# Layer 1's norm and the reading of the top-k maxima move from VectorE to GpSimd in a four-stage block on one core

## The reference

```
def _L1_xattn_ref(query, key, value, Wq, Wk):
    ...
    scores = jnp.einsum('bhqa,bhka->bhqk', q, k) * SCALE
    top_vals = jax.lax.top_k(scores, TOP_K)[0]
    cutoff = top_vals[..., -1:]
    masked = jnp.where(scores >= cutoff, scores, -jnp.inf)
    w = jax.nn.softmax(masked, axis=-1)
    e = jnp.einsum('bhqk,bhka->bhqa', w, v)
...
x = x + _L0_xattn_ref(_layernorm(x, axis=-1), ctx_1024, ctx_1024, mask_BxS2_bf1, ...)
x = x + _L0_ffn_ref(_layernorm(x, axis=-1), ...)
x = x + _L1_xattn_ref(_layernorm(x, axis=-1), ctx_1024, ctx_1024, L1_xattn_Wq, L1_xattn_Wk)
x = x + _L1_ffn_ref(_layernorm(x, axis=-1), ...)
```

## Time and profile before

| | us |
|---|---|
| median of three runs | 620.87 |
| the profiled execution | 620.93 |
| its span, first to last instruction | 618.9 |
| VectorE busy | 513.5 |
| TensorE busy | 443.1 |
| ScalarE busy | 280.4 |
| GpSimd busy | 255.2 |

### The profile page before, as it was taken

How to read it: one execution, slowest core, us unless ns; L and a number is a source line. 1 busy time by engine, 2 the same in 40 slices (tenths; PEclk the granted TensorE clock), 3 DMA queues, 4 the chain that set the end, 5 groups by cost and what they waited for, 6 DMA issues and landing times.

```text
span 618.9 us, 10023 instructions
## 1 busy us (share of the span) xinstructions
PE 443.1 (72%) x2321; PEld 334.7 (54%) x2321; DVE 513.5 (83%) x3073; ACT 280.4 (45%) x781; POOL 255.2 (41%) x388
## 2 busy tenths in 40 slices
PE   5879978687877877637777757765977876556355
PEld 4458755466664764524656535654755655445244
DVE  5845776947884998999875999999999999989971
ACT  2213431321232424522674758676567877443521
POOL 5400110500131255342672765675486776444611
PEclk9999995957677668755876779789568978566555
DMA  8500000000000000000000000000000000000000
GB/s 294 215 1 1 2 2 0 0 1 1 2 0 1 2 1 0 2 1 2 5 2 5 5 2 2 10 2 1 6 5 6 3 9 3 5 5 5 5 1 8
DMA packets 5929, 9.54 MB, mean 15 GB/s; under 512 B 744, under 2 KB 4976, under 8 KB 5616
## 3 DMA queue, kind: packets, MB, share of 16 engines
q1 hardware_dynamic: 5584, 8.35, 3.8%
q10 hardware_dynamic: 288, 0.56, 0.3%
HBM read 7.86 MB, written 1.05 MB: 14 GB/s over the span
## 4 chain that ended last, share of the span: by engine, by line
PE 38%; DVE 37%; ACT 11%; issue 9%; POOL 3%; DMA 1%; SPq 0%; ACTq 0%; DVEq 0%; POOLq 0%
DVE area_b L921 10%; DVE top L913 9%; PE psM L1261 5%; PE psM L1066 4%; PE psM L1211 3%; PE psM L1203 3%; ACT mparts L557 2%; DVE mxc L928 2%; PE psS L1034 2%; PE psM L1198 2%; PE psM L1139 2%; DVE d L691 2%; PE psT L1055 2%; PE psT L1247 2%; PE psS L1037 2%
## 5 line engine op out<-in xcount | busy, mean ns | idle before, releaser
L913 DVE MAX8 top<-area_b 128x8 f32<-128x77 f32 x768 | 112.4, 221 | 0.0
L921 DVE MATCH_REPLACE8 area_b<-top,area_b 128x77 f32<-128x77 f32 x512 | 106.9, 222 | 0.0
L307 POOL TENSOR_TENSOR rstd_m<-veps_m,expo 128x4 f32<-128x4 f32 x8 | 8.1, 1013 | 130.7 <-DVE veps_m L659 130.7
L1261 PEld LDWEIGHTS psM<-vblk,pT 128*128 128x128 f32 (+1 forms) x320 | 52.5, 256 | 11.6 <-issue 10.5
L1261 PE MATMUL psM<-vblk,pT 128*128 128x81 f32 (+1 forms) x320 | 53.9, 341 | 6.1 <-ACT pT L612 5.8
L1066 PE MATMUL psM<-vblk,pT 128*128 128x81 f32 (+1 forms) x320 | 49.1, 320 | 6.9 <-DVE x L712 3.4
L921 DVE MATCH_REPLACE8 area_b<-top,area_a 128x77 f32<-128x77 f32 x256 | 53.5, 224 | 0.0
L1066 PEld LDWEIGHTS psM<-vblk,pT 128*128 128x128 f32 (+1 forms) x320 | 47.5, 236 | 10.4 <-issue 10.1
L408 POOL TENSOR_TENSOR p<-area_b 128x1232 f32<-128x1232 f32 x15 | 41.9, 2793 | 21.8 <-issue 17.1
L1203 PE MATMUL psM<-w,y1T 128*128 128x512 f32 (+1 forms) x64 | 34.1, 624 | 20.0 <-ACT mparts L557 19.8
L1247 PE MATMUL psT<-consts,p 128*128 128x128 f32 (+1 forms) x160 | 34.3, 342 | 19.5 <-ACT pT L608 10.5
(11 more groups left out here) (220 smaller groups left out, 1074.9 us busy)
## 6 DMA issues: line engine op xcount, KB each, us to landing
area_a<-in_w1T SPq DMA_DIRECT2D x1, 2064.0 KB, 11.2
area_b<-in_w SPq DMA_DIRECT2D x1, 2048.0 KB, 15.7
x<-in_x SPq DMA_DIRECT2D x4, 256.0 KB, 6.8
out<-fin SPq DMA_DIRECT2D x16, 64.0 KB, 1.6
rows<-in_rows SPq DMA_DIRECT2D x1, 576.0 KB, 6.9
vblk<-in_vblk SPq DMA_DIRECT2D x1, 540.0 KB, 15.6
weights<-in_weights SPq DMA_DIRECT2D x1, 516.0 KB, 6.7
consts<-in_consts ACTq DMA_DIRECT2D x1, 392.5 KB, 4.0
```

The source lines that it names most:

```text
L913: ins = e.max(top[:, r, h], (left if r else scores_sb[t % RING])[:, h])
L921: ins = e.match_replace(left[:, h], top[:, r, h], (left if r else scores_sb[t % RING])[:, h], GONE)
L1261: ins = mm(pvs1[:, :, FIRST[c] * VE:FIRST[c] * VE + VB], pT1[0:w, c], vblk1[0:w, t // NJ, c, None, :].broadcast_to([w, COPIES, VB]), start ...
```

## The change

Four edits:

1. `top` has two buffers, by the tile's parity. `mxc` and the copies `free` and `ends` are gone. GpSimd's `dif` and `cut` read the maxima in `top` itself, and wait for the steps of the top-k. The first MAX8 of tile t waits for the cut subtraction of tile t-2 (`cut_set` at t-1), where it waited for the previous tile's copy.
2. The step `norm` of tiles 0 to 14 is GpSimd's. A new ScalarE step, `ncopy`, copies the product, 128 x 144, to `avs` in SBUF, and GpSimd raises the 16 sums to the power -1 (`inverse` holds -1) and multiplies. Tile 15 keeps VectorE's norm.
3. In ORDER, `ncopy@t` stands right before `norm@t`, and `free` and `ends` are taken out. All other steps stand as they stood.
4. GpSimd sets the constant `inverse` at the start.

```diff
-        top = sb("top", [P, TOPK // 8, H, 8])
-        mxc = sb("mxc", [P, RING, 2, H])
+        top = sb("top", [P, 2, TOPK // 8, H, 8])
...
+        avs = sb("avs", [P, H, VE])
+        inverse = sb("inverse", [P, H])
...
+            e.memset(inverse[:], -1.0).then_inc(s["constants_set"], 1)
...
                 def a():
-                    hold(e, s["S_read"], t + 1)
+                    hold(e, s["topk_step"], TOPK_STEPS * t + G)
                     hold(e, s["exp_set"], t)
-                    e.tensor_tensor(dif[:], scores_sb[t % RING][:], mxc[:, t % RING, 0, :, None].broadcast_to([P, H, KEYS]), ALU.subtract)\
+                    e.tensor_tensor(dif[:], scores_sb[t % RING][:], top[:, t % 2, 0, :, 0, None].broadcast_to([P, H, KEYS]), ALU.subtract)\
...
-                    hold(e, s["mx_copied"], t + 1)
-                    e.tensor_tensor(cut, scores_sb[t % RING][:], mxc[:, t % RING, 1, :, None].broadcast_to([P, H, KEYS]), ALU.subtract)\
+                    hold(e, s["topk_step"], TOPK_STEPS * t + TOPK_STEPS)
+                    e.tensor_tensor(cut, scores_sb[t % RING][:], top[:, t % 2, TOPK // 8 - 1, :, 7, None].broadcast_to([P, H, KEYS]), ALU.subtract)\
...
             def value(t):
+                def norm():
+                    hold(e, s["constants_set"], 7)
+                    hold(e, s["a_copied"], t + 1)
+                    e.tensor_tensor(rden1[:], avs[:, :, HD], inverse[:], ALU.pow).then_inc(s["a_den"], 1)
+                    hold(e, s["a_den"], t + 1)
+                    hold(e, s["x3_set"], t)
+                    e.tensor_tensor(att1.rearrange("p (h d) -> p h d", h=H), avs[:, :, 0:HD],
+                                    rden1[:, :, None].broadcast_to([P, H, HD]), ALU.mult).then_inc(s["a_norm"], 1)
...
                 def keep():
                     hold(e, s["S_ready"], t + 1)
-                    hold(e, s["S_read"], t + 1 - RING)
...
+            def value(t):
+                def aside():
+                    hold(e, s["a_made"], t + 1)
+                    hold(e, s["a_norm"], t)
+                    e.activation(avs[:], pv1, ACT.Copy).then_inc(s["a_copied"], 1)
+                return dict(ncopy=aside) if t < LASTT else {}
...
                         if r == 0:
-                            hold(e, s["mx_copied"], t)
+                            hold(e, s["cut_set"], t - 1)
                             hold(e, s["S_kept"], t + 1)
...
-                def free():
-                    hold(e, s["cut_set"], t + 1 - RING)
-                    hold(e, s["topk_step"], last(2))
-                    e.tensor_copy(mxc[:, t % RING, 0], top[:, 0, :, 0]).then_inc(s["S_read"], 1)
-
-                def ends():
-                    hold(e, s["topk_step"], last(2 * rounds - 1))
-                    e.tensor_copy(mxc[:, t % RING, 1], top[:, rounds - 1, :, 7]).then_inc(s["mx_copied"], 1)
```

## The result

| kernel | median us (range, runs) | ratio to before, 95% interval | profiled execution, its span |
|---|---|---|---|
| before | 620.44 (618.68 to 620.9, 4) | | 620.93, 618.9 |
| changed | 651.90 (650.41 to 656.38, 4) | 1.0525, [1.0469, 1.058] | 650.41, 648.6 |

The change costs 31.5 us by the medians and 29.7 us by the spans. 648 us was forecast, and 617 to 662 as the range. (One line of the change isn't in the diff ahead: TensorE's next product with the values waits for ScalarE's copy and no longer for the norm.)

A forecast was written before the change was run, and what follows sets the result against it. VectorE was taken to set the pace only in part, with GpSimd, ScalarE and TensorE nearly as late in fixed order. Terms 7.6 + 6.5 + 14.0 + 2.4 = 30.5 us, less an eighth, +27: 648 us, range 617 to 662.

The forecast's parts named there:

- The power: GpSimd's power of 128x16 in each norm of tiles 0 to 14: 2.87 us by the line through one and four columns.
- (b): Rival: the power costs about 1.0 us at 16 columns, as at four, giving 624 us; chance 0.12.
- What VectorE loses: Both small copies of the maxima and the norm of 15 tiles leave VectorE: 27.6 us of its time.
- The multiply and the copy: In each moved norm, GpSimd's multiply of 128x128 takes 0.45 us and ScalarE's copy of the product 0.30 us.
- Tiles 0 and 1: +7.6: Start of tile 4's top-k comes 7.6 us later: tile 1 +3.8, tile 0 +3.5, tile 2's new copy +0.3.
- Tiles 2 to 6: +6.5: Up to tile 7's cut: five norms add 17.0 us, less 10.5 of vanishing waits for VectorE.
- Tiles 7 to 11: +14.0: Each norm costs its 3.3 us less the slack between x3's add and ScalarE's sum; together 14.0 us.
- Tiles 12 to 14: +2.4: Loop from cut to cut becomes 21.5 us: +3.1 from tile 12 to 13, -0.7 from 13 to 14.
- The eighth: Estimated deduction from the 30.5 us sum, for idle time of ScalarE and GpSimd from 450 to 500 us; leaves +27.
- (a): Rival: VectorE sets the end and the queues absorb the norms; 604 us, or 596 if early norms hide too; chance 0.17.
- (c): Rival: only the loop from cut to cut counts, the queues have room for the rest; 619 us; chance 0.09.
- (d): Rival: TensorE, waiting more, keeps its lower clock from tile 7 on, adding some 10 us; 658 us; chance 0.08.

The follow-up runs named there:

- three lengths of it: Changed kernel with GpSimd's power over 4 of 16 columns, over all 16, or done twice: 623.52, 651.90 and 700.19 us.
- the one with tiles 0 to 6: Maxima read in place in all tiles, norm on GpSimd only in tiles 0 to 6 and on VectorE in 7 to 14: 629.46 us, ratio 1.0151 to the kernel before.
- three buffers: Changed kernel with a third buffer for the maxima, so the first MAX8 waits for the cut of tile t-3: 651.83 us, ratio 1.054 to the kernel before.
- the table of the halves: Kernel before with only the maxima read in place: 610.77 us; with only the norm moved to GpSimd: 655.29 us; the table adds combined and split-tile kernels.
- the same power beside the chain: Maxima in place, norm on VectorE, plus a GpSimd power of constants that nothing waits for: 626.94 us, ratio 1.0112 to the kernel before.

## Why the prediction was right, point by point

**The power.** The line through one and four columns gave 2.87 us, the trace has 2.92. This term carries the case, and the rival of a cheap power (b) fell with it. Its price for one us of power, about one us of the end, is what three lengths of it showed.

**What VectorE loses.** 27.6 us were forecast, and 26.0 came off. The long copies of the earlier trace rows lie beside another instruction of GpSimd than the subtraction that the prediction named: in the kernel before, the longest starts at 430.46 us and ends with GpSimd's multiply of exp and sign (timelines of VectorE and GpSimd), and six of the seven copies over 1.5 us lie beside that multiply.

```profile
430.46 2.52 DVE L928 COPY mxc<-top 128x16 f32<-128x16 f32 x1
```

```profile
430.17 2.78 POOL L408 TENSOR_TENSOR p<-area_b 128x1232 f32<-128x1232 f32 x1 [0.85 <-ACT area_b L600]
```

**The multiply and the copy.** 0.45 and 0.30 us were taken, 0.405 and 0.293 measured. The Trainium skill (GPSIMD Engine Reference, section 4.1) has two-input work on GpSimd at about twice VectorE's time; here the same multiply is 0.405 us on GpSimd and 0.291 on VectorE, 1.4 times. No run moves the multiply alone. With multiply and copy moved and the reciprocal on VectorE, 9 us stay, and 15 times the 0.11 us between the two multiplies is 1.7 of them.

**Tiles 0 and 1: +7.6.** Right: +7.3 in three of the four profiles with this code, and +7.1 in all four at tile 3's scores, where the prediction's two terms for tiles 0 and 1 give 7.3. Tile 4's first MAX8, forecast at 347 and not 339 us, came at 340.6 in the profile of the changed kernel, where TensorE's clock had given 5 us back, and at 344.5 in the one with tiles 0 to 6, whose layer 1 had begun 2.4 us earlier than that of the kernel before: 346.9 when counted as in the earlier trace rows.

**Tiles 2 to 6: +6.5.** Wrong by 9 to 10 us. The five norms cost 16.8 us (15.2 with three buffers), where I had put 17.0 before any deduction. The step that failed is the deduction of 10.5 us for waits for VectorE that would vanish. (Its 4.3 us are moreover those of all fifteen cuts.) They did vanish: GpSimd's idle time before the cuts and the adds of x3 fell from 43.3 us to 1.3. But 48.4 us before the power, for ScalarE's copy of the product, took their place. By the table of the halves this stretch takes 102.2 us with the norm on GpSimd, whether VectorE has its small copies to do or not (103.8 in the profile of the changed kernel), and 87.0 and 82.1 us with the norm on VectorE: the relief is worth 4.9 us beside VectorE's norm and nothing beside GpSimd's.

**Tiles 7 to 11: +14.0.** 10.8 measured, and not in the portions of 1.8 to 3.3 us a tile that were forecast. From cut to cut the changed kernel takes 7.2 and 7.3 us more where two norms lie between (tiles 9 to 10 and 11 to 12), 0.7 less where one does (7 to 8), and 1.0 and 2.0 less where none does. That the slack between add and sum sets these, as the prediction had it, isn't shown.

**Tiles 12 to 14: +2.4.** 1.0 measured. The loop is the one foreseen: the cuts stand 22.2 and 21.5 us apart where 21.5 was forecast, +3.8 and -0.7. From tile 14's cut to the end the changed kernel takes 2.1 us less, where nothing was forecast; why, wasn't looked into (timeline, GpSimd; against the earlier trace rows):

```profile
562.76 2.26 POOL L404 TENSOR_TENSOR area_b<-area_a,top 128x1232 f32<-128x1232 f32 x1
...
584.99 2.26 POOL L404 TENSOR_TENSOR area_b<-area_a,top 128x1232 f32<-128x1232 f32 x1
...
606.50 2.26 POOL L404 TENSOR_TENSOR area_b<-area_a,top 128x1232 f32<-128x1232 f32 x1
```

**The sum.** 30.5 us before the deduction, 27 with it, against 29.7 by the spans, 30.8 by the count from the first scores, and 31.5 by the medians. The eighth that I took off for idle time on ScalarE and GpSimd made it worse: with the power in the chain, no run shows that idle time paid for it. But that the 30.5 come so close is luck: a stretch too small by 10 us stands beside the 5 us of the clock, 3 us of tiles 7 to 11 and 1.4 of the end. In the profile with three buffers, where the clock gave nothing back, the count is +33.5.

**The rivals.** (a), VectorE sets the end, is half true of the kernel before: its top-k is on the chain there, and 19 us less work on it are worth 8. It wasn't true of the changed kernel, in which an earlier VectorE earned nothing. (c), only the loop counts, fell: the norms of tiles 0 to 6 alone cost 18.7 us. (d), a lower clock of TensorE, was small: 0.81 granted from 450 to 500 us against 0.84 before, and 0.53 against 0.57 from 550 to 600, in a stretch that added 1 us. Over the whole profiled execution it was 0.724 against 0.755; how much of the 30 us comes with that, no run sets apart.

## What to carry to other kernels

When engines hand one item of work round in a fixed order, price a moved operation by its length on its new engine times how often it stands in that round, and don't set against it the waits on the engine it leaves: those are offsets only if the chain runs through them. Here that price held on the average over the tiles, and it held for work in the chain: the same power beside the chain cost 0.37 us for each us of its length. VectorE was busy for 99% of 50 us, and yet the kernel gained less than half of what was taken off it. And look for a second loop through the same operation before moving it out of the first.

## What the runs showed of the hardware that I had not expected

- GpSimd's power grows evenly with the columns: 0.549 us at 128x1 (exponent -0.5), 1.02 at 128x4 and 2.92 at 128x16 (exponent -1), so 0.16 us a column, while its multiply of 128x128 takes 0.41 us. VectorE's reciprocal of the same 128x16 takes 0.25 us.
- GpSimd's subtraction of 128x1232 takes 2.265 us when it reads its 16 broadcast values in place from the maxima, one of each 8, and 2.248 when they lie together: 0.5 us over all 31 of them. Costing it at nothing was fair.
- The same code up to tile 4 ran with two grants of TensorE's clock, 0.79 or 0.50 to 0.53 from 320 to 340 us, and the difference of 5 us that went with it is as large as one of the terms of the sum. One profile isn't enough to judge a term of that size.
